# Two GNN layers on one core: the first norm remade in fp32 by ScalarE, z loaded by GpSimd's queue, the second projection and the first gate group in parts of rows

## The reference, cut to what matters

```
xn = _layernorm(x, axis=-1)
x  = x + _L0_gnn_ref(xn, ...) + _L0_mix_ref(xn[None], ...)[0]
x  = x + _L0_ffn_ref(_layernorm(x)[None], ...)[0]

# _L0_gnn_ref
u = _rgcn(x, edge_index, edge_type, weight, root, bias)   # eight relations
z = jnp.concatenate([u, x], axis=1) @ w_gate + b_gate
h = jnp.tanh(u) * z + x * (1.0 - z)
# _L0_mix_ref ends with
return out @ W_proj.T + b_proj
```

## Time and profile before

| | us |
|---|---|
| median of 3 runs | 1987.85 (1986.59 to 1988.09) |
| profiled execution | 1984.67, its span 1983.3 |
| TensorE busy | 1846.9 (93%) |
| VectorE busy | 1103.9 (56%) |
| GpSimd busy | 735.2 (37%) |
| ScalarE busy | 443.8 (22%) |
| mean granted TensorE clock | 0.965 of full |

### The profile page before, as it was taken

One profiled execution on the slowest core, in us unless ns is written; L12 is line 12 of the kernel. 1 busy time (PEld: TensorE's weight loads), 2 busy tenths in 40 slices (PEclk: granted clock), 3 DMA queues, 4 the chain that ended last, 5 costly groups with the idle time before them and its releaser, 6 DMA issues.

```text
span 1983.3 us, 28492 instructions
## 1 busy us (share of the span) xinstructions
PE 1846.9 (93%) x9601; PEld 1453.9 (73%) x9601; DVE 1103.9 (56%) x2729; ACT 443.8 (22%) x1016; POOL 735.2 (37%) x626
## 2 busy tenths in 40 slices
PE   6999999999999999999999998554999999999999
PEld 4876667767777878778787776443788888877777
DVE  7889999987454353544525279876632224262121
ACT  3239955551111010110101131121100001111010
...
DMA packets 107298, 162.63 MB, mean 82 GB/s; under 512 B 8108, under 2 KB 43108, under 8 KB 106940
## 3 DMA queue, kind: packets, MB, share of 16 engines
...
## 4 chain that ended last, share of the span: by engine, by line
PE 78%; DVE 12%; ACT 5%; DVEq 2%; issue 2%; DMA 1%; SPq 0%; ACTq 0%
PE ps L364 20%; PE ps L365 19%; PE ps L366 19%; PE ps L1178 8%; PE ps L819 3%; ACT sc_col L765 2%; ACT sc_row L764 1%; PE ps L2113 1%; PE ps L1143 1%; PE ps L1585 1%; DVE w_lo L297 1%; DVE stats L318 1%; PE ps L1115 1%; PE ps L808 1%; ACT w_hi L292 1%
## 5 line engine op out<-in xcount | busy, mean ns | idle before, releaser
L364 PE MATMUL ps<-w_hi,xt_hi 128*125 128x512 f32 (+1 forms) x1800 | 752.6, 418 | 27.9 <-DVE ring L428 7.7
L365 PE MATMUL ps<-w_lo,xt_hi 128*125 128x512 f32 (+1 forms) x1800 | 710.9, 395 | 0.0
L366 PE MATMUL ps<-w_hi,xt_lo 128*125 128x512 f32 (+1 forms) x1800 | 708.9, 394 | 0.0
L249 POOL TENSOR_TENSOR w_hi<-w_stage,zero 128x512 fp32r<-128x512 f32 x280 | 313.6, 1120 | 836.4 <-PE ps L366 722.7
L364 PEld LDWEIGHTS ps<-w_hi,xt_hi 128*125 128x125 f32 x1800 | 338.2, 188 | 105.5 <-issue 16.4
L366 PEld LDWEIGHTS ps<-w_hi,xt_lo 128*125 128x125 f32 x1800 | 337.4, 187 | 84.3
L252 POOL TENSOR_TENSOR w_lo<-w_stage,w_hi 128x512 fp32r<-128x512 f32 x280 | 387.6, 1384 | 22.0
L365 PEld LDWEIGHTS ps<-w_lo,xt_hi 128*125 128x125 f32 x1800 | 338.2, 188 | 69.2
L276 POOL DMA_DIRECT2D pre<-ring x45 | 24.4, 543 | 338.5 <-DVE ring L428 335.9
L1178 PE MATMUL ps<-a_hi,xn_hi 125*128 125x313 f16 (+1 forms) x640 | 106.7, 297 | 1.0 <-DVE mtmp L1316 1.0
L1178 PE MATMUL ps<-a_hi,xn_lo 125*128 125x313 f16 (+1 forms) x640 | 106.3, 297 | 0.0
...
## 6 DMA issues: line engine op xcount, KB each, us to landing
w_stage<-in_stream SPq DMA_DIRECT2D x374, 256.0 KB, 2.7
...
```

Of the source, the lines that this page charges most:

```text
L249: POOL.tensor_tensor(w_hi[:, q, :], w_stage[:, q % NST, :], zero[:].to_broadcast([128, 512]), ALU.add).then_inc(S("hi_done"), 1)
L364: PE.matmul(dst, l_hi, r_hi, start=first, stop=False)
L365: PE.matmul(dst, l_hi, r_lo, start=False, stop=False)
L366: return PE.matmul(dst, l_lo, r_hi, start=False, stop=last)
```

## The change

1. **fp32 norm.** VectorE keeps rs, rs + 1 and -mean x rs of the first norm (`r_first`, `r_first1`, `m_first`) by three small operations. ScalarE's new `norm_again(m)` writes xn of a row tile in fp32 (`xn32`, in the place of xn_hi and xn_lo) and turns x1 of that tile into x + xn in place. Tiles 0 and 1 stand behind ao's feed 4, tiles 2 to 4 behind feed 7. VectorE's `add_xn` goes; the bias is added per row tile, and `less_xn` is one operation instead of two.
2. **z.** SP's two loads of z and their wait go; GpSimd issues them when it has split the first projection group's chunks and all of ao is turned.
3. **Splitting.** Chunks of the second projection group and of both gate groups get their high half from ScalarE and only their low half from GpSimd.
4. **Parts.** Projection group 1 and gate group 0 are made for row tiles 0 and 1 first, over all eight chunks, and then for tiles 2 to 4. Feeds 8 to 15 stand in the second part of projection group 1. TensorE waits for all of them at once ahead of gate group 0.
5. **Order.** The rounding, clipping and bf16 copies of the weights stand ahead of the feeds; VectorE evacuates tiles 0 and 1 of projection group 1 ahead of the feeds, tiles 2 to 4 behind the last.

```diff
--- before.py
+++ after.py
@@ -127,7 +127,7 @@
     rs = small("rs", [P, T], F32)
     t5 = small("t5", [P, T], F32)
     dis = small("dis", [P, T], F32)
-    rs_first = small("rs_first", [P, T], F32)
+    r_first, r_first1, m_first = (small(n, [P, T], F32) for n in ("r_first", "r_first1", "m_first"))
     flag = small("flag", [128, 1], F32)
     flag_i = small("flag_i", [128, 1], I32)
     gam = small("gam", [128, 2], F32)
@@ -261,6 +261,8 @@
 
     C_HAND, C_BACK = 32, 86
 
+    z = at("z", [P, T, D], F32, R_A)
+
     def split_low(c, q):
 
         POOL.wait_ge(S("hi_done"), c + 1)
@@ -279,7 +281,12 @@
     POOL.wait_ge(S("rcnt"), 1)
     for c in range(C_BACK, C_BACK + (-C_BACK) % NSL):
         split_chunk(c, c % NSL, c // NST + 1)
-    split_rounds(C_BACK + (-C_BACK) % NSL, C_L1)
+    split_rounds(C_BACK + (-C_BACK) % NSL, C_PROJ + KT)
+    POOL.wait_ge(S("feed_full"), KT)
+    for g in range(2):
+        POOL.dma_start(z[:, :, g * 512:(g + 1) * 512], pre[2 + g].rearrange("t p f -> p t f")).then_inc(S("ld_z"), 16)
+    for c in range(C_PROJ + KT, C_L1):
+        split_low(c, c % NSL)
     POOL.wait_ge(S("split_done"), NST + C_L1 + NSL)
     split_rounds(C_L1 + NSL, nloop * NSL)
     for c in range(nloop * NSL, NSTREAM):
@@ -397,6 +404,21 @@
                 elif k == KT - 1:
                     last.then_inc(S("bank_full"), 1)
 
+    def dense_part(c0, g0, rows, behind):
+
+        for k in range(KT):
+            PE.wait_ge(S("split_done"), NST + c0 + k + 1)
+            for m in rows:
+                if k == 0:
+                    PE.wait_ge(S("bank_free"), g0 * T + m + 1)
+                last = three(ps[0:P, m, :], xt_hi[:, k, m * P:(m + 1) * P], xt_lo[:, k, m * P:(m + 1) * P],
+                             w_hi[:, k, :], w_lo[:, k, :], k == 0, k == KT - 1)
+                if m == T - 1:
+                    last.then_inc(S("w_used"), 1)
+                elif k == KT - 1:
+                    last.then_inc(S("bank_full"), 1)
+            behind(k)
+
     def wait_bank(eng, g, m, c0, g0):
 
         if m < T - 1:
@@ -519,6 +541,9 @@
     first_norm(4)
     first_low(3)
     first_low(4)
+    DVE.tensor_copy(r_first[:], rs[:])
+    DVE.tensor_scalar(r_first1[:], rs[:], 1.0, None, ALU.add)
+    DVE.scalar_tensor_tensor(m_first[:], mv[:, :, 0], -1.0, rs[:], ALU.mult, ALU.mult)
 
     first_dev(0)
     first_dev(1)
@@ -983,7 +1008,6 @@
     eps_t = at("a0_eps", [P, 1], F32, R_EARLY + 2784)
     qft = qt[:, 0, :]
     ao = at("ao", [P, T, D], F32, R_A)
-    z = at("z", [P, T, D], F32, R_A)
     x1 = at("x1", [P, T, D], F32, R_A + T * D * 4)
     w1 = at("w1", [128, KT, FFN0], F32, R_EXTRA)
     w2 = at("w2", [128, FFN0 // 128, D], F32, R_EXTRA + 8192)
@@ -1038,10 +1062,6 @@
         if c == C_PROJ + 4:
             SP.dma_start(bias_p[:], a["bias"][B_PROJ0:B_PROJ0 + 2, :].rearrange("(o g) f -> o g f", o=1).to_broadcast(
                 [P, 2, 512])).then_inc(S("ld_bp"), 16)
-        if c in (C_PROJ + 12, C_PROJ + 14):
-            g = (c - C_PROJ - 12) // 2
-            SP.wait_ge(S("feed_full"), KT)
-            SP.dma_start(z[:, :, g * 512:(g + 1) * 512], pre[2 + g].rearrange("t p f -> p t f")).then_inc(S("ld_z"), 16)
         if c == C_GATE + 4:
             SP.wait_ge(S("wq_done"), 2)
             SP.dma_start(lng[:], a["ln_g"].to_broadcast([P, D])).then_inc(S("ld_ln"), 16)
@@ -1233,6 +1253,14 @@
         ALE.wait_ge(S("a0_C"), r + 1)
         ALE.activation(qft[:, 0:C1], ps[:, 5, 0:C1], ACT.Copy).then_inc(S("a0_Ca"), 1)
 
+    xn32 = at("xn32", [P, T, D], F32, R_XN)
+
+    def norm_again(m):
+
+        ALE.activation(xn32[:, m, :], x1[:, m, :], ACT.Identity, scale=r_first[:, m:m + 1], bias=m_first[:, m:m + 1])
+        ALE.activation(x1[:, m, :], x1[:, m, :], ACT.Identity, scale=r_first1[:, m:m + 1],
+                       bias=m_first[:, m:m + 1]).then_inc(S("x_again"), 1)
+
     with ALE.Fori(0, REL - 1) as r:
         relation_act(r)
         ALE.wait_ge(S("a0_Dd"), r + 2)
@@ -1245,6 +1273,12 @@
     mk_deg = sig(ALE.activation(t5[:], va[:], ACT.Sqrt), "act_step")
     for k in range(KT):
         feed_act(k, k)
+        if k == 4:
+            ALE.wait_ge(S("ld_res"), 16 * T)
+            norm_again(0)
+            norm_again(1)
+    for m in (2, 3, 4):
+        norm_again(m)
 
     def counts_dve(r):
 
@@ -1373,34 +1407,41 @@
         if m == T - 1 and k < 3:
             feed_pe(ao, 5 + k, 5 + k)
 
-    def proj_second(k, m):
-        if (k, m) == (0, T - 1):
+    def proj_second(k):
+        if k == 0:
             PE.wait_ge(S("rgam"), 1)
-        if m == T - 1:
-            feed_pe(nat, k, KT + k)
+        feed_pe(nat, k, KT + k)
 
     dense_pe(0, c0, g0, lambda k: PE.wait_ge(S("feed_lo"), k + 1), proj_first)
     PE.wait_ge(S("gsum"), 1)
     PE.matmul(ps[:, 7, 504:506], ones[:], gsum[:], start=True, stop=True, skip_group_check=True).then_inc(S("gam"), 1)
-    dense_pe(1, c0, g0, None, proj_second)
-    dense_pe(0, c1, g1, lambda k: PE.wait_ge(S("feed_lo"), KT + k + 1))
+    dense_part(c0 + KT, g0 + 1, (0, 1), lambda k: None)
+    dense_part(c0 + KT, g0 + 1, (2, 3, 4), proj_second)
+    PE.wait_ge(S("feed_lo"), 2 * KT)
+    for rows in ((0, 1), (2, 3, 4)):
+        dense_part(c1, g1, rows, lambda k: None)
     dense_pe_rows(1, c1, g1)
 
 
     MAGIC = 1.5 * 2.0 ** 23
+    ALE.wait_ge(S("split_done"), NST + C_PROJ + KT)
+    for c in range(C_PROJ + KT, C_GATE):
+        split_act(c)
     ALE.wait_ge(S("rgam"), 1)
     for i, w in enumerate((w1, w2)):
         wf = w[:].rearrange("p k f -> p (k f)")
         ALE.activation(wf, wf, ACT.Copy, scale=rgam[:, i:i + 1], bias=MAGIC).then_inc(S("w_round"), 1)
+    for i, (w, wq) in enumerate(((w1, w1q), (w2, w2q))):
+        ALE.wait_ge(S("w_clip"), i + 1)
+        ALE.activation(wq[:].rearrange("p k f -> p (k f)"), w[:].rearrange("p k f -> p (k f)"), ACT.Copy,
+                       bias=-MAGIC).then_inc(S("wq_done"), 1)
     for k in range(KT):
         kc = slice(k * 128, (k + 1) * 128)
         feed_act(k, KT + k)
         ALE.activation(nat[:, :, kc], nat[:, :, kc], ACT.Tanh).then_inc(S("tanh"), 1)
-        if k < 2:
-            w, wq = ((w1, w1q), (w2, w2q))[k]
-            ALE.wait_ge(S("w_clip"), k + 1)
-            ALE.activation(wq[:].rearrange("p k f -> p (k f)"), w[:].rearrange("p k f -> p (k f)"), ACT.Copy,
-                           bias=-MAGIC).then_inc(S("wq_done"), 1)
+        split_act(C_PROJ + 2 * KT + k)
+    for c in range(C_GATE + KT, C_L1):
+        split_act(c)
 
 
     newton_after(mk_deg)
@@ -1411,58 +1452,46 @@
     for i, w in enumerate((w1, w2)):
         DVE.tensor_reduce(gsum[:, i:i + 1], w[:].rearrange("p k f -> p (k f)"), AX.X, ALU.add, apply_absolute_value=True)
     DVE.drain().then_inc(S("gsum"), 1)
-    DVE.wait_ge(S("ld_res"), 16 * T)
     DVE.wait_ge(S("ld_bp"), 16)
-    for g in range(2):
-        o = x1[:, :, g * 512:(g + 1) * 512]
-        DVE.tensor_tensor(o, o, bias_p[:, g, :].unsqueeze(1).to_broadcast([P, T, 512]), ALU.add)
+    for m in range(T):
+        DVE.wait_ge(S("x_again"), m + 1)
+        o = x1[:, m, :]
+        DVE.tensor_tensor(o, o, bias_p[:].rearrange("p g f -> p (g f)"), ALU.add)
     DVE.drain()
 
-    def add_xn(m):
-
-        DVE.tensor_tensor(x1[:, m, :], x1[:, m, :], xn_hi[:, m, :], ALU.add)
-        DVE.drain()
-        DVE.tensor_tensor(x1[:, m, :], x1[:, m, :], xn_lo[:, m, :], ALU.add)
-        DVE.drain()
-
-    add_xn(0)
-    add_xn(1)
-
-    def proj_evac(g):
-
-        for m in range(T):
-            wait_bank(DVE, g, m, c0, g0)
-            o = x1[:, m, g * 512:(g + 1) * 512]
-            DVE.tensor_tensor(o, o, ps[0:P, m, :], ALU.add).then_inc(S("bank_free"), 1)
+    def proj_evac(g, m):
+
+        wait_bank(DVE, g, m, c0, g0)
+        o = x1[:, m, g * 512:(g + 1) * 512]
+        DVE.tensor_tensor(o, o, ps[0:P, m, :], ALU.add).then_inc(S("bank_free"), 1)
 
     def less_xn(k):
 
         kc = slice(k * 128, (k + 1) * 128)
         DVE.wait_ge(S("tanh"), k + 1)
-        DVE.tensor_tensor(nat[:, :, kc], nat[:, :, kc], xn_hi[:, :, kc], ALU.subtract)
-        DVE.drain()
-        DVE.tensor_tensor(nat[:, :, kc], nat[:, :, kc], xn_lo[:, :, kc], ALU.subtract)
-
-    proj_evac(0)
+        DVE.tensor_tensor(nat[:, :, kc], nat[:, :, kc], xn32[:, :, kc], ALU.subtract)
+
+    for m in range(T):
+        proj_evac(0, m)
     DVE.wait_ge(S("gam"), 1)
     DVE.tensor_scalar(gam[:], ps[:, 7, 504:506], 1.0 / (FFN0 * D), 1e-5, ALU.mult, ALU.add)
     DVE.drain()
     DVE.reciprocal(rgam[:], gam[:])
     DVE.drain().then_inc(S("rgam"), 1)
+    for i, w in enumerate((w1, w2)):
+        DVE.wait_ge(S("w_round"), i + 1)
+        wf = w[:].rearrange("p k f -> p (k f)")
+        DVE.tensor_scalar(wf, wf, MAGIC - 1.0, MAGIC + 1.0, ALU.max, ALU.min).then_inc(S("w_clip"), 1)
+    for m in (0, 1):
+        proj_evac(1, m)
     for k in range(KT):
         feed_dve(k, KT + k)
-        if k < 2:
-            DVE.wait_ge(S("w_round"), k + 1)
-            wf = (w1, w2)[k][:].rearrange("p k f -> p (k f)")
```

(9 more changed lines are left out.)

12 lines of the change are left out of this document (removed).

## The result

| | before | changed |
|---|---|---|
| median of 4 runs, us | 1987.74 (1986.59 to 1988.09) | 1967.81 (1966.85 to 1970.01) |
| profiled execution, us | 1984.67, span 1983.3 | 1970.01, span 1968.6 |

The ratio is 0.9902 with a 95% interval of 0.9885 to 0.9919: the changed kernel is 19.9 us faster. The forecast was 1972.4, so 15.5 faster, with a range of 1967.5 to 1981.0. The median lies 0.3 us inside that range.

The account below looks back on a forecast made before the run. TensorE, busy 93%, and its waits bound the path to the second gate group's first evacuation. Arrival -15.8 and small norm operations +0.3 gave -15.5 us: 1987.85 to 1972.4, range 1967.5 to 1981.

Parts of the forecast that it names:

- The path up to the arrival: TensorE from first projection group's end to second gate group's first evacuation: 83.86 us before, arrival 15.8 sooner, at 1230.7.
- second projection with feeds: Second projection group, tiles 0 and 1 first, feeds beside tiles 2 to 4: 32.08 us against 34.65.
- wait behind the feeds: TensorE's wait ahead of the gate for the last feed's low halves: 1.86 us against 4.97, clock staying up.
- gate group 0 and row tile 0: First gate group 27.72 us, second group's row tile 0 5.54; VectorE's evacuations put the arrival at 1230.7.
- The stage behind: From the second gate group's first evacuation to TensorE's next work at 1289.24: VectorE's 42.7 us, length kept.
- The front's +0.3: VectorE's three small operations in the first norm: cost 0.3 us, bounds 0 and 0.8.
- the carry from the trace to the median: Whole kernel: median taken as 3.2 us above the profiled execution, making 1969.2 into 1972.4.
- my +5: Bound on z in GpSimd's queue: a second-projection chunk late behind z could cost 5 us; expected cost 0.
- The feeds set no turn: Rival denied: feeds in the second projection hold turns at 3.41 us, gain only 7.3, 1980.6; chance 0.12.
- Late chunks: Rival: loads or low halves late in the second projection, costing 5 + 1.9 us, gain 8.6, 1979.3; chance 0.08.
- The clock did not fall in the turns: Rival denied: TensorE's clock stays down in eight turns and first gate group, 29 us slower, 2017; chance 0.04.
- The stage behind 1289: Rival: the stage there waits for something fixed in time, so the gain vanishes, 1987.9; chance 0.02.

Follow-up runs that it names:

- e10: The kernel before, unchanged, run and traced a second time: 1986.49 us, ratio 1.000.
- e5: The changed kernel, unchanged, run and traced a second time: 1966.49 us, ratio 0.9899 to the kernel before.
- e4: The changed kernel with z loaded by SP again, ahead of chunks 220 and 222: 1973.37 us, ratio 0.9933 to the kernel before.
- e3: The changed kernel with the subtraction of xn made twice per feed: 1972.8 us, ratio 0.9932 to the kernel before.
- e6: The changed kernel without parts of rows, weights' clipping and bf16 copies back between the feeds: 1979.58 us, ratio 0.9964 to the kernel before.
- e8: The kernel before with only the fp32 norm of the change: 1975.45 us, ratio 0.9940 to the kernel before.

## Why the prediction was right, and where it was short

**The path up to the arrival** came out term by term. From the end of the first projection group (1162.5); the first row lies ahead of it:

| term | forecast, us | measured, us |
|---|---|---|
| bias additions of five tiles | 7.5, done near 1160 | 9.07, done at 1160.4 |
| wait for bank 0 | 0 | 0 |
| second projection with feeds | 32.08 | 32.39 (to 1196.61 - 1.75) |
| wait behind the feeds | 1.86 | 1.75 |
| gate group 0 and row tile 0 | 33.3, VectorE ready at 1230.7 | 33.5; VectorE starts at 1230.42, having idled 0.19 for TensorE |
| a turn with a feed | 2.62 | 2.62 |

That the clock would stay up behind 1.86 us held, but the argument for it was weak. I had compared the waits of 2.02 and 4.97 alone. The same trace has waits of 0.8, 1.7 and 1.0 for low halves between 1239 and 1245 and, from 1242 on, twelve matmuls at the lower level (the 0.79 of the earlier trace rows), and behind a wait of 2.44 at 1131 eight. The arrival moved by 16.13 us where 15.8 were forecast. VectorE did not bound it: its three tiles took 7.05 us (1223.37 to 1230.42), not 7.6, since GpSimd lengthened an addition only in the first (1.20 instead of 0.69).

**The stage behind** was forecast to keep its 42.7 us; it took 42.09 (1230.42 to 1272.51), 0.6 less.

**The front's +0.3** can't be seen: ao's fifth feed ends at 1128.8 against 1128.9, but the same point lay at 1126.2 in the second trace of the kernel before (e10).

**That the range held, by 0.3 us, is luck.** The 1967.8 lies below the 1969 to 1976 that the forecast had for itself, and the changed kernel's second median (1966.5, e5) lies below both.

**The step that failed is the last one, the carry from the trace to the median.** I took the median to be 3.2 above the traced execution for both kernels. It was 2.2 below it in the changed one: 1967.8 against 1970.0. By the traces alone the gain is 14.7, with 16.7 at the first work behind the long wait and 2.0 lost to a fall at 1900 (e5). By two traces of each it is (160.4 + 162.1)/2 - 143.7 = 17.6 for the stretch. The runs say 19.9 and 20.5. Each trace of the kernel before happened to be shorter than its median by 1 to 3 us; the first has no fall near its wait of 2.41 at 1916, where the changed kernel's first trace has one at 1900. One or two falls of the clock make such a difference; that they are it was not shown for the untraced runs, so 2 to 3 us of the 20 stay open.

**Costed at nothing, and not nothing: z.** The prediction gave the move to GpSimd's queue 0, since before nobody paid for SP's stall. With parts somebody would have: e4 makes it 4.8 us of stretch, 6.4 with the fall. The mechanism behind my +5, a chunk late behind z, is what e4 showed, with z in the queue it left. Chunk 220 did land 9.6 us after ScalarE asked, and its low half ended at 1166.4, where TensorE wanted it at 1168. Rounding then began at 1168.9, five microseconds behind the scales, and the last copy of the weights ended at 1176.4, where I had 1173.5 and the first feed's transposes start at 1175.8. ScalarE took that feed at 1176.5 and TensorE paid nothing, but the 2.4 us of slack that I had there were gone:

```profile
1151.42 1.23 ACT L1261 ACTIVATE x<-x,m_first,r_first 125x1024 f32<-125x1024 f32 x1
...
1164.35 0.64 ACT L299 ACTIVATE w_hi<-w_stage 128x512 fp32r<-128x512 f32 x1 [9.62 <-DMA w_stage<-in_stream]
...
1168.88 3.89 ACT L1433 ACTIVATE w<-w,rgam 128x2048 f32<-128x2048 f32 x2
...
1174.47 1.89 ACT L1436 ACTIVATE w2q<-w 128x2048 bf16<-128x2048 f32 x1
...
1177.28 1.28 ACT L1441 ACT_TABLE_LOAD   x1
```

```profile
1145.38 3.37 POOL L287 DMA_DIRECT2D z<-pre  x2 [14.66 <-PE ps L1108]
```

The times from issue to landing, of z's two halves and of the chunks beside them:

```profile
DMA to landing us min/median/max: 6.6/13.8/21.1
```

```profile
w_stage<-in_stream SPq DMA_DIRECT2D x7, 256.0 KB, 6.6
```

The Trainium skill warns (SBUF — State Buffer, SBUF: two separate sides) that VectorE can keep GpSimd from writing descriptors. No stall of the issue shows: the two took 3.37 us together beside low halves and a reduction of VectorE. But the warning is for VectorE's 2-port perf-mode operations, and no row tells that one ran then, so this is no test of it. The Trainium skill also says (DMA: Bandwidth & Descriptors, Issuing engines are not separate DMA queues) that transfers of all issuing engines run interleaved on the same DMA engines. The trace agrees: z's two halves took 6.6 and 21.1 us to land, and a chunk in that time a median of 6.6, against 2.7.

**Rivals.** The feeds set no turn (2.62 held, VectorE idle 1.0 in each), and e3 shows how near it was: with one operation more VectorE meets GpSimd's low half and the turn is 3.0. Late chunks cost nothing, by 1.0 to 1.7 us of slack. The clock did not fall in the turns (1.00 from 1165 to 1250). The stage behind 1289 did not swallow the gain.

**What the parts are worth** the prediction never asked alone. The norm gives 9.8 us by itself. In parts, ScalarE's halves and z's new queue are worth 5 to 7 each; without parts the two together cost 1.5 to 3 us of the stretch and 4 us in the runs (e6 against e8, which does not tell them apart). The edits are one change: parts make TensorE take the second projection's chunks up to three times as fast (1.39 us against 4.01), and the other two pay for that.
